# Another order for the rounds of a graph attention: where VectorE's and TensorE's pieces of work stand between the links of a chain

## The chip, the cores and the metric

One core of one Trainium2 chip runs the whole kernel as one program. The metric is device time in microseconds; the kernel before was run three times, 1138.68, 1143.45 and 1144.17 us, so its median is 1143.45 us. One more execution was recorded by the hardware profiler; it took 1135.31 us, with a span of 1133.6 us from the first to the last instruction.

## The reference

The reference is one layer of a graph network on 3125 nodes of 256 features and 50000 edges, sorted by their destination node. Three parts are added to the input: an attention over the edges, a linear attention over all nodes, and a mixture of eight experts. Only the first is touched here:

```
q = (feats @ Wq.T + bq)   k = (feats @ Wk.T + bk)   v = (feats @ Wv.T + bv)     # 8 heads of 32
qe = q[:, c, :]    ke = k[:, r, :]    ve = v[:, r, :]      # r: source, c: destination of each edge
sim = einsum('hed,hed->eh', qe, ke) * scale
m = segment_max(sim, c)          p = exp(sim - m[c])       s = segment_sum(p, c)
out_e = (p / s[c]) * ve          agg = segment_sum(out_e, c)
return agg @ Wo.T + bo
```

So for each edge and each head there is a product of the destination's query with the source's key, a softmax over the edges that share a destination, and a weighted sum of the sources' values.

## The kernel before, in words

The program has stages one after another: preparation (projections, tables of the edges), the linear attention, the edge attention (function `attention`, from about 200 to 815 us), and the end with the experts. The five engines each have an instruction stream of their own, which runs in the order in which it is written, and they meet by semaphores only. There is no scheduler: the order of the code is the order on the engine.

In `attention` the edges are cut into 28 chunks of 16 steps of 128 edges (the last chunk has 8 steps). A step is one row of tiles: 128 edges on the partitions, all in the window of one block of 125 nodes. Four steps are a turn (q = 0 to 3), so a chunk has four turns. For each turn the work is:

- GpSimd gathers the keys and values of the source nodes with 4 indirect DMAs (L968) into one of ten ring places.
- `turned_hots(n)` on VectorE (L1048) makes the one-hot matrix hotT of a whole chunk; `spread_q(n, q)` on TensorE (12 matmuls, L1194) multiplies it with the node queries, so that each edge has its query in the PSUM tile at_pq (two of them, by turns).
- `product(n, q)` on VectorE (L1054) multiplies at_pq with the gathered keys, `reduce(n, q)` (L1061) sums each head: the scores.
- `turn_scores(c)` on TensorE transposes the scores of a chunk, and a chain of small steps finds the maximum of each node's edges, also across rows and chunks: `local_maxima` (two scans on VectorE, L1096 and L1098), `ends` (two transposes on TensorE), a copy on ScalarE (at_row, L1022), `carries` (two scans of one row and three small operations on VectorE, L1102 to L1107), `columns` (TensorE L1221, then VectorE's copy L1111), `maxima` (L1115, L1117, L1119), the exponential on ScalarE (L1030), `turn_weights` and `factor` on TensorE (L1227, L1232).
- `weigh(c, q)` on VectorE (L1070) multiplies the values with the weights into at_pv; `sums(c, q)` on TensorE (two groups of 4 matmuls, L1204) sums over the edges of each node; `add(c, q, i)` on VectorE (L1084) adds each group's result to the node sums agg; `rescale(c)` (L1092) multiplies a node's sums when its maximum has grown.

ScalarE also makes the one-hot matrices at_hot for `sums` (L988, L991).

A round n works on three chunks at once: the scores of chunk n, the chain and the first two turns of the sums of chunk c = n - 1, and the last sums of chunk b = n - 2. The order of the pieces within a round is written out by hand in the function `body` of each engine. Two things set what may start: `spread_q(n, q)` may overwrite a tile at_pq only when the product two turns back is done, and group p of `sums` may overwrite its tile only when the add two groups back is done. `windows(c, q)` loads the numbers of the node blocks of a turn from a table into registers (L929, TENSOR_LOAD); the instructions that address agg by them (add and rescale) have a short register instruction ahead (shown as ISA).

Of the kernel before, what the change touches and what calls it, by code (L numbers as in the profile page):

```python
# [862 lines left out]
def attention(nc, m):  # L863
# [7 lines left out]
    with ExitStack() as ctx:  # L871
# [43 lines left out]
        def exists(c, q=0):  # L915

            return not isinstance(c, int) or (0 <= c < CH and q < quads(c))
# [15 lines left out]
        with nc.Block() as block:  # L933
# [109 lines left out]
            def _(dve):  # L1043
# [65 lines left out]
                def columns(c):  # L1109
                    dve.wait_ge(S.chain_pe, CHAIN_PE * c + PE_COLUMNS)  # L1110
                    dve.tensor_copy(col[:, :], pc[:, 384:386]).then_inc(S.chain, 1)  # L1111
# [9 lines left out]
                def body(n):  # L1121
                    c, b = n - 1, n - 2
                    if exists(b, 2):
                        weigh(b, 2)
                    if exists(b, 1):
                        wins = windows(b, 1)
                        add(b, 1, 0, wins)
                    if exists(n, 0):
                        product(n, 0)
                    if exists(b, 1):  # L1130
                        add(b, 1, 1, wins)
                    if exists(c):
                        local_maxima(c)
                    if exists(n, 0):
                        reduce(n, 0)
                    if exists(c):
                        carries(c)

                    if exists(b, 3):
                        weigh(b, 3)  # L1140
                    if exists(b, 2):
                        wins = windows(b, 2)
                        add(b, 2, 0, wins)
                    if exists(c):
                        columns(c)
                    if exists(b, 2):
                        add(b, 2, 1, wins)
                    if exists(c):
                        maxima(c)
                    if exists(n, 1):  # L1150
                        product(n, 1)
                        reduce(n, 1)

                    if exists(c, 0):
                        weigh(c, 0)
                    if exists(b, 3):
                        wins = windows(b, 3)
                        add(b, 3, 0, wins)
                    if exists(n, 2):
                        product(n, 2)  # L1160
                    if exists(b, 3):
                        add(b, 3, 1, wins)
                    if exists(n, 2):
                        reduce(n, 2)
                    if exists(c):
                        wins = windows(c, 0)
                        rescale(c, wins[0])

                    if exists(c, 1):
                        weigh(c, 1)  # L1170
                    if exists(c, 0):
                        add(c, 0, 0, wins)
                    if exists(n) and exists(n + 1):
                        turned_hots(n + 1)
                    if exists(c, 0):
                        add(c, 0, 1, wins)
                    if exists(n, 3):
                        product(n, 3)
                        reduce(n, 3)
                turned_hots(0)  # L1180
                dve.wait_ge(S.at_const, AT_CONST)
# [4 lines left out]
            def _(pe):  # L1186
# [47 lines left out]
                def windows(c, q):  # L1234
                    return windows_of(c, slice(2 * q, 2 * q + 2), PE_ONLY)

                def body(n):
                    c, b = n - 1, n - 2
                    if exists(n, 1):
                        wins = windows(n, 1)  # L1240
                    if exists(n, 1):
                        spread_q(n, 1, wins)
                    if exists(n, 2):
                        wins = windows(n, 2)
                    if exists(c):
                        turn_scores(c)
                    if exists(b, 2):
                        sums(b, 2)
                    if exists(c):
                        ends(c)  # L1250

                    if exists(c):
                        columns(c)
                    if exists(n, 2):
                        spread_q(n, 2, wins)
                    if exists(n, 3):
                        wins = windows(n, 3)
                    if exists(b, 3):
                        sums(b, 3)
                    if exists(c):  # L1260
                        turn_weights(c)
                        factor(c)

                    if exists(n, 3):
                        spread_q(n, 3, wins)
                    if exists(n) and exists(n + 1):
                        wins = windows(n + 1, 0)
                    if exists(c, 0):
                        sums(c, 0)

                    if exists(c, 1):
                        sums(c, 1)
                    if exists(n) and exists(n + 1):
                        spread_q(n + 1, 0, wins)
                pe.wait_ge(S.at_const, AT_CONST)
                spread_q(0, 0, windows_of(0, slice(0, 2), PE_ONLY))
                for n in range(CH + 2):
# [598 lines left out]
```

## Time and profile before

| | us |
|---|---|
| median of three runs (1138.68 to 1144.17) | 1143.45 |
| profiled execution | 1135.31 |
| its span | 1133.6 |
| VectorE busy | 867.7 |
| TensorE busy (matmul) | 893.9 |
| GpSimd busy | 586.7 |
| ScalarE busy | 484.7 |

The span is longer than any engine's busy time because the stages have different limits. VectorE is busy for 90% and more in the slices of the attention and for less than half in the experts, TensorE is busy for 70 to 80% in the attention and for over 90% in the experts. The mean clock granted to TensorE is 0.916 of full speed over the whole span. A matmul's busy time includes the time in which it overlaps the next, so a sum of such times is no measure of work.

### The profile page before, as it was taken

What the parts mean: (1) busy time and instruction counts of PE and PEld (TensorE: products, weight loads), DVE (VectorE), ACT (ScalarE), POOL (GpSimd) and SP (SyncE); (2) the same over time, 40 slices, a digit from 0 to 9 for tenths busy, and PEclk for the clock granted to TensorE, in tenths of its full rate; (3) what the DMA queues carried; (4) which work ended last, traced back from release to release, by engine and by line L of the source; (5) the groups of instructions that cost most, each with busy time, mean ns of one, the idle gap of its engine ahead of it and who ended that gap; (6) DMA issues with size and microseconds to landing.
All of it is one profiled execution on the core that took longest, in us unless ns stands there. A gap on an engine that the chain in (4) does not pass through costs nothing. (4 is left out here: it accounts for less than half of the span.)

```text
span 1133.6 us, 15267 instructions
## 1 busy us (share of the span) xinstructions
PE 893.9 (79%) x4059; PEld 618.0 (55%) x4059; DVE 867.7 (77%) x1760; ACT 484.7 (43%) x1312; POOL 586.7 (52%) x635
## 2 busy tenths in 40 slices
PE   4889967578777777777877877777685599999995
PEld 3445543356556555555555655555453366666664
DVE  3787877799999999999999999999578134444444
ACT  3566436454455454445445445544332232232330
POOL 2533467767777777777777777771001323232311
PEclk9989969788998988999989899997887799999998
DMA  5334265468777777777677676671231443333300
GB/s 147 107 98 112 78 178 153 146 188 216 217 203 210 213 204 189 191 199 201 184 199 194 176 197 181 174 201 44 68 111 63 132 149 120 103 121 114 111 11 9
DMA packets 79878, 167.46 MB, mean 148 GB/s; under 512 B 15514, under 2 KB 47005, under 8 KB 79549
## 3 DMA queue, kind: packets, MB, share of 16 engines
q0 software_dynamic: 38464, 110.26, 36.2%
q1 hardware_dynamic: 39431, 54.81, 15.6%
q10 hardware_dynamic: 1904, 1.45, 0.4%
q8 instruction: 35, 0.57, 0.2%
q14 instruction: 44, 0.36, 0.1%
HBM read 163.32 MB, written 18.95 MB: 161 GB/s over the span
## 5 line engine op out<-in xcount | busy, mean ns | idle before, releaser
L968 POOL DMA_INDIRECT slot<-kv_d,src_e x320 | 322.8, 1009 | 116.3 <-issue 91.7
L1204 PE MATMUL at_pa<-at_pv,at_hot 128*125 128x264 f32 x880 | 268.0, 446 | 81.4 <-DVE agg L1084 80.5
L1204 PEld LDWEIGHTS at_pa<-at_pv,at_hot 128*125 128x125 f32 x880 | 173.6, 213 | 155.1 <-DVE agg L1084 126.4
L988 ACT ACTIVATE at_hot<-iota_w,nloc_e 128x125 f32<-128x125 f32 x440 | 138.9, 386 | 132.8 <-PE at_pa L1204 132.6
L1194 PE MATMUL at_pq<-q,at_hotT 125*128 x1320 | 172.2, 287 | 16.0 <-issue 10.9
L1194 PEld LDWEIGHTS at_pq<-q,at_hotT 125*128 125x128 bf16 x1320 | 130.5, 102 | 44.5 <-issue 20.5
L1061 DVE TENSOR_REDUCE at_sc<-at_prod 128x32 f32<-128x1024 f32 x110 | 133.4, 1213 | 2.0
L1635 DVE TENSOR_TENSOR y<-xp,b 128x256 f32<-128x256 f32 (+1 forms) x32 | 13.6, 425 | 138.3 <-PE xp L1681 138.3
L1614 POOL DMA_INDIRECT out<-slot,node_s x32 | 32.1, 1004 | 166.0 <-DVE slot L1646 135.3
L1054 DVE TENSOR_TENSOR at_prod<-at_pq,slot 128x1024 f32<-128x1024 f32 x88 | 107.0, 1216 | 9.3 <-PE at_pq L1194 7.0
L1681 PE MATMUL xp<-slot,hm 128*128 128x256 f32 (+1 forms) x512 | 113.1, 379 | 0.0
L1070 DVE TENSOR_TENSOR at_pv<-slot,at_pp 128x1056 f32<-128x1056 f32 x88 | 109.3, 1242 | 0.0
L1671 PE MATMUL xp<-extra,slot 128*128 128x489 f32 x256 | 108.2, 581 | 0.8 <-ACT extra L1579 0.8
L1681 PEld LDWEIGHTS xp<-slot,hm 128*128 128x128 f32 (+1 forms) x512 | 94.3, 185 | 18.2 <-issue 3.5
L1084 DVE TENSOR_TENSOR agg<-agg,at_pa 125x264 f32 x220 | 92.4, 420 | 8.0 <-PE at_pa L1204 3.0
L1590 ACT ACTIVATE hm<-xp,b 128x489 f32<-128x489 f32 x64 | 42.9, 670 | 114.2 <-PE xp L1671 114.2
L991 ACT ACTIVATE at_hot<-at_hot,one_col 128x500 f32<-128x500 f32 x110 | 78.3, 712 | 3.6
L1671 PEld LDWEIGHTS xp<-extra,slot 128*128 128x128 f32 x256 | 49.3, 193 | 55.5 <-issue 49.7
L1221 PE MATMUL at_pchain<-at_one_c,at_line 1*128 1x1 f32 x112 | 17.3, 254 | 48.2 <-DVE at_line L1105 48.2
L631 PE MATMUL pa<-slot,xnT 128*125 128x512 f32 x100 | 51.1, 637 | 3.8 <-DVE vst L438 3.8
L968 POOL DMA_INDIRECT base<-kv_d,src_e x44 | 44.5, 1012 | 14.2 <-issue 12.3
L968 POOL DMA_INDIRECT extra<-kv_d,src_e x44 | 44.0, 1001 | 14.7 <-issue 12.8
(319 smaller groups left out, 1318.4 us busy)
## 6 DMA issues: line engine op xcount, KB each, us to landing
slot<-in_w SPq DMA_DIRECT2D x16, 1024.0 KB, 7.6
locrow<-loc_d SPq DMA_DIRECT2D x28, 500.0 KB
slot<-kv_d,src_e POOLq DMA_INDIRECT x352, 4.0
kv_d<-vst SPq DMA_DIRECT2D x25, 128.9 KB
base<-in_x SPq DMA_DIRECT2D x5, 625.0 KB
kv_d<-kst SPq DMA_DIRECT2D x25, 125.0 KB
row_d<-base SPq DMA_DIRECT2D x5, 625.0 KB
out<-base SPq DMA_DIRECT2D x1, 3125.0 KB
```

The costliest lines, as they stand in the source:

```text
L631: mm = pe.matmul(dst[par][0:TT, 0:b - a], xnT[:, par, c, :], wall[:, c, a:b], start=(c == 0), stop=(c == 1))
L968: pool.indirect_dma_start(m.quads[r][:, i, :], None, m.kv_d, bass.IndirectOffsetOnAxis(ap=m.src_e[:, c, u:u + 1].bitcast(U32), axis=0), bo ...
L988: last = act.activation(hot[:, u % 8, :], m.iota_w[:, :], ACT.Abs, bias=at(m.nloc_e, c)[:, u:u + 1])
L991: act.activation(hot[:, four, :], hot[:, four, :], ACT.Relu, bias=m.one_col[:, 0:1], scale=-1.0).then_inc(S.hot_made, 1)
L1054: dve.tensor_tensor(prod[:, :, :], pq[q % 2].rearrange("p (i d) -> p i d", i=4), m.quads[place(n, q)][:, :, 0:D], ALU.mult).then_inc(S.pro ...
L1061: dve.tensor_reduce(sc[:, :, 4 * q:4 * q + 4].rearrange("p h i -> p i h"), prod.rearrange("p i (h d) -> p i h d", h=H), X, ALU.add).then_i ...
L1070: dve.tensor_tensor(pv[:, 4 * (q % 2):4 * (q % 2) + 4, :, :], m.quads[place(c, q)][:, :, D:KV].rearrange("p i (h c) -> p i h c", h=H), spr ...
L1084: dve.tensor_tensor(dst, dst, pa[p % 2][:, 0:H * VW].rearrange("p (h c) -> p h c", h=H), ALU.add).then_inc(S.added, 1)
L1194: mm = pe.matmul(pq[q % 2][:, u * D:(u + 1) * D], hotT[:, 4 * q + u, :], at(m.q3, wins[u // 2])[:, part, :], start=(part == 0), stop=(part ...
L1204: mm = pe.matmul(pa[p % 2][:, 0:H * VW], hot[:, u % 8, :], pv[:, u % 8, :, :].rearrange("p h c -> p (h c)"), start=(u % 2 == 0), stop=(u % ...
L1671: mm = pe.matmul(p1[f % 2][:, 0:CAP], w1[par][:, c, f * 128:(f + 1) * 128], hT[par][:, c, 0:CAP], start=(c == 0), stop=(c == 1))
L1681: mm = pe.matmul(p2[i % 2][0:sizes[i], 0:D], hm[:, f, 128 * i:128 * i + sizes[i]], w2[par][:, f, :], start=(f == 0), stop=(f == FC - 1))
```

## The change

The functions that do the work are not touched. In the rounds of VectorE, `carries(c)` moves behind `weigh(b, 3)` and the first add of turn 2, `product(n, 1)` and `reduce(n, 1)` move ahead of `columns(c)` and `maxima(c)` and have an add between them, the adds of turn 3 follow `maxima(c)` at once, `turned_hots(n + 1)` moves ahead of `weigh(c, 0)`, `weigh(c, 0)` moves behind it, and `product(n, 3)` and `reduce(n, 3)` have an add between them. In the rounds of TensorE, `turn_scores(c)` goes ahead of `spread_q(n, 1)`, `ends(c)` ahead of `sums(b, 2)`, `columns(c)` goes behind `spread_q(n, 2)`, `turn_weights(c)` and `factor(c)` behind `spread_q(n, 3)`, and `spread_q(n + 1, 0)` ahead of `sums(c, 0)`.

```diff
--- before.py
+++ after.py
@@ -1131,28 +1131,27 @@
                         add(b, 1, 1, wins)
                     if exists(c):
                         local_maxima(c)
+
                     if exists(n, 0):
                         reduce(n, 0)
-                    if exists(c):
-                        carries(c)
-
                     if exists(b, 3):
                         weigh(b, 3)
                     if exists(b, 2):
                         wins = windows(b, 2)
                         add(b, 2, 0, wins)
                     if exists(c):
-                        columns(c)
+                        carries(c)
+
+                    if exists(n, 1):
+                        product(n, 1)
                     if exists(b, 2):
                         add(b, 2, 1, wins)
+                    if exists(n, 1):
+                        reduce(n, 1)
                     if exists(c):
+                        columns(c)
                         maxima(c)
-                    if exists(n, 1):
-                        product(n, 1)
-                        reduce(n, 1)
-
-                    if exists(c, 0):
-                        weigh(c, 0)
+
                     if exists(b, 3):
                         wins = windows(b, 3)
                         add(b, 3, 0, wins)
@@ -1162,20 +1161,23 @@
                         add(b, 3, 1, wins)
                     if exists(n, 2):
                         reduce(n, 2)
+                    if exists(n) and exists(n + 1):
+                        turned_hots(n + 1)
+
+                    if exists(c, 0):
+                        weigh(c, 0)
                     if exists(c):
                         wins = windows(c, 0)
                         rescale(c, wins[0])
-
                     if exists(c, 1):
                         weigh(c, 1)
                     if exists(c, 0):
                         add(c, 0, 0, wins)
-                    if exists(n) and exists(n + 1):
-                        turned_hots(n + 1)
+                    if exists(n, 3):
+                        product(n, 3)
                     if exists(c, 0):
                         add(c, 0, 1, wins)
                     if exists(n, 3):
-                        product(n, 3)
                         reduce(n, 3)
                 turned_hots(0)
                 dve.wait_ge(S.at_const, AT_CONST)
@@ -1238,40 +1240,39 @@
                     c, b = n - 1, n - 2
                     if exists(n, 1):
                         wins = windows(n, 1)
+                    if exists(c):
+                        turn_scores(c)
                     if exists(n, 1):
                         spread_q(n, 1, wins)
                     if exists(n, 2):
                         wins = windows(n, 2)
                     if exists(c):
-                        turn_scores(c)
+                        ends(c)
                     if exists(b, 2):
                         sums(b, 2)
-                    if exists(c):
-                        ends(c)
-
-                    if exists(c):
-                        columns(c)
+
                     if exists(n, 2):
                         spread_q(n, 2, wins)
                     if exists(n, 3):
                         wins = windows(n, 3)
+                    if exists(c):
+                        columns(c)
                     if exists(b, 3):
                         sums(b, 3)
-                    if exists(c):
-                        turn_weights(c)
-                        factor(c)
-
                     if exists(n, 3):
                         spread_q(n, 3, wins)
                     if exists(n) and exists(n + 1):
                         wins = windows(n + 1, 0)
+                    if exists(c):
+                        turn_weights(c)
+                        factor(c)
+
+                    if exists(n) and exists(n + 1):
+                        spread_q(n + 1, 0, wins)
                     if exists(c, 0):
                         sums(c, 0)
-
                     if exists(c, 1):
                         sums(c, 1)
-                    if exists(n) and exists(n + 1):
-                        spread_q(n + 1, 0, wins)
                 pe.wait_ge(S.at_const, AT_CONST)
                 spread_q(0, 0, windows_of(0, slice(0, 2), PE_ONLY))
                 for n in range(CH + 2):
```

The first place is on VectorE, from the carries' end to the first add of turn 3 (agg<-agg,at_pa is an add, at_prod a product, at_sc a reduce, at_pv a weigh, win_of the table of windows). Before:

```order
L1111 COPY at_col<-at_pchain 128x2 [waits chain_pe]
L1084 ISA [waits added,summed]
L1084 TENSOR_TENSOR agg<-agg,at_pa 125x264
L1115 SCALAR_TENSOR_TENSOR at_fwd_max<-edge,at_col,at_pchain 128x128 [waits chain]
L1117 SCALAR_TENSOR_TENSOR at_back_max<-at_bwd_st,at_col,at_fwd_max 128x128 [waits chain]
L1119 TENSOR_TENSOR at_back_max<-at_pchain,at_back_max 128x128 [waits chain]
L1054 TENSOR_TENSOR at_prod<-at_pq,extra 128x1024 [waits reduced,q_spread,arrived9]
L1061 TENSOR_REDUCE at_sc<-at_prod 128x4x8 [waits prod_made]
L1070 TENSOR_TENSOR at_pv<-slot,at_pp 128x1056 [waits summed,chain_pe]
L929 TENSOR_LOAD win_of
L1084 ISA [waits added,summed]
L1084 TENSOR_TENSOR agg<-agg,at_pa 125x264
```

and now, from the reduce of turn 1 on:

```order
L1061 TENSOR_REDUCE at_sc<-at_prod 128x4x8 [waits prod_made]
L1111 COPY at_col<-at_pchain 128x2 [waits chain_pe]
L1115 SCALAR_TENSOR_TENSOR at_fwd_max<-edge,at_col,at_pchain 128x128 [waits chain]
L1117 SCALAR_TENSOR_TENSOR at_back_max<-at_bwd_st,at_col,at_fwd_max 128x128 [waits chain]
L1119 TENSOR_TENSOR at_back_max<-at_pchain,at_back_max 128x128 [waits chain]
L929 TENSOR_LOAD win_of
L1084 ISA [waits added,summed]
L1084 TENSOR_TENSOR agg<-agg,at_pa 125x264
L1054 TENSOR_TENSOR at_prod<-at_pq,slot 128x1024 [waits reduced,q_spread,arrived0]
```

The table load (L929) stood behind a product, a reduce and a weigh; now it stands directly behind the three instructions of maxima, each of which waits on the semaphore `chain` for the one before, and the adds that need it come next.

The second place is on VectorE too, in the second half of a round, about hotT. Before:

```order
L1061 TENSOR_REDUCE at_sc<-at_prod 128x4x8 [waits prod_made]
L929 TENSOR_LOAD win_of
L1092 ISA [waits added,chain_pe]
L1092 TENSOR_TENSOR agg<-agg,at_pchain 125x264
L1070 TENSOR_TENSOR at_pv<-slot,at_pp 128x1056 [waits summed]
L1084 TENSOR_TENSOR agg<-agg,at_pa 125x264 [waits added,summed,rescaled]
L1048 TENSOR_SCALAR at_hotT<-locrow,iota_p 125x2048 [waits q_spread,loc_in]
L1084 ISA [waits added,summed,rescaled]
L1084 TENSOR_TENSOR agg<-agg,at_pa 125x264
```

and now:

```order
L1061 TENSOR_REDUCE at_sc<-at_prod 128x4x8 [waits prod_made]
L1048 TENSOR_SCALAR at_hotT<-locrow,iota_p 125x2048 [waits q_spread,loc_in]
L1070 TENSOR_TENSOR at_pv<-slot,at_pp 128x1056 [waits summed,chain_pe]
L929 TENSOR_LOAD win_of
L1092 ISA [waits added,chain_pe]
L1092 TENSOR_TENSOR agg<-agg,at_pchain 125x264
L1070 TENSOR_TENSOR at_pv<-slot,at_pp 128x1056 [waits summed]
L1084 TENSOR_TENSOR agg<-agg,at_pa 125x264 [waits added,summed,rescaled]
L1054 TENSOR_TENSOR at_prod<-at_pq,slot 128x1024 [waits reduced,q_spread,arrived1]
L1084 ISA [waits added,summed,rescaled]
L1084 TENSOR_TENSOR agg<-agg,at_pa 125x264
```

hotT stood between the two adds of turn 0 of chunk c, behind weigh and rescale; now it stands ahead of the weigh, and two weighs and the rescale are all that is between it and the first of those adds.

The third place is on TensorE, from the turn of the weights to the turn of the scores (at_pp is the turned weights, at_pchain<-at_fall the factor, at_pq a spread, at_pa sums; each spread has twelve matmuls, and rows that repeat are left out). Before:

```order
L1227 MATMUL at_pp<-ident,at_back_max 128x128 [waits pv_made,chain_act]
L1232 MATMUL at_pchain<-at_fall,at_pair 125x8 [waits chain,chain_act]
L1194 ISA [waits prod_made]
L1194 MATMUL at_pq<-q,at_hotT 128x256
...
L929 TENSOR_LOAD win_of
L1204 MATMUL at_pa<-at_pv,at_hot 125x264 [waits pv_made,hot_made,added]
L1204 MATMUL at_pa<-at_pv,at_hot 125x264
...
L1204 MATMUL at_pa<-at_pv,at_hot 125x264 [waits pv_made,hot_made,added]
...
L1194 ISA [waits prod_made,hotT_made]
```

and now:

```order
L1229 MATMUL at_pp<-ident,at_back_max 128x128 [waits pv_made,chain_act]
L1234 MATMUL at_pchain<-at_fall,at_pair 125x8 [waits chain,chain_act]
L1196 ISA [waits prod_made,hotT_made]
L1196 MATMUL at_pq<-q,at_hotT 128x256
...
L1206 MATMUL at_pa<-at_pv,at_hot 125x264 [waits pv_made,hot_made,added]
L1206 MATMUL at_pa<-at_pv,at_hot 125x264
...
L1206 MATMUL at_pa<-at_pv,at_hot 125x264 [waits pv_made,hot_made,added]
...
L1213 MATMUL at_pchain<-ident,at_sc 128x128 [waits rescaled,reduced]
L1196 ISA [waits prod_made]
```

Before, the spread that waits for hotT stood behind the sums of turns 0 and 1; now it stands ahead of them, and they can't start until it has been through. Line numbers on TensorE are two higher in the changed kernel.

## Rows read from the trace of the kernel before

**Rows 1.** The instructions on the tile hotT in the attention (xcount: ns min/median/max, first and last start).

```profile
L1048 DVE TENSOR_SCALAR at_hotT<-locrow,iota_p x26: 744/758/768, 234.4 to 775.1; 125x2048 bf16<-125x2048 bf16 x26
```

**Rows 2.** Busy time by engine in 25 rounds (stretch, length, busy us (x count), clock, DMA).

```profile
234.40:775.10 540.70, 417.39 (x2250) 303.45 (x2250) 523.18 (x826) 263.48 (x728) 400.57 (x398) 0.93 0.73 197
```

**Rows 3.** VectorE's waits in that stretch (waiting line <- releaser: us, times, longest).

```profile
DVE at_run L1102 <- ACT at_row L1022: 4.6, 10, 0.5
DVE at_prod L1054 <- issue: 2.8, 10, 0.4
```

**Rows 4.** VectorE's timeline, about one round (start us, us, instruction).

```profile
537.99 0.75 DVE L1048 TENSOR_SCALAR at_hotT<-locrow,iota_p 125x2048 bf16<-125x2048 bf16 x1
...
544.99 1.19 DVE L1061 TENSOR_REDUCE at_sc<-at_prod 128x32 f32<-128x1024 f32 x1
546.30 0.45 DVE L1102 TENSOR_TENSOR_SCAN at_run<-at_stop,at_row 1x144 f32<-1x144 bf16 x1
...
549.06 0.14 DVE L1111 COPY at_col<-at_pchain 128x2 f32<-128x2 f32 x1
549.34 0.43 DVE L1084 TENSOR_TENSOR agg<-agg,at_pa 125x264 f32 x1
549.69 0.47 DVE L1115 TENSOR_TENSOR_SCAN at_fwd_max<-edge,at_col,at_pchain 128x128 f32<-128x128 bf16 x1
...
550.72 0.29 DVE L1119 TENSOR_TENSOR at_back_max<-at_pchain,at_back_max 128x128 f32<-128x128 f32 x1
550.93 1.22 DVE L1054 TENSOR_TENSOR at_prod<-at_pq,slot 128x1024 f32<-128x1024 f32 x1
552.18 1.22 DVE L1061 TENSOR_REDUCE at_sc<-at_prod 128x32 f32<-128x1024 f32 x1
553.31 1.24 DVE L1070 TENSOR_TENSOR at_pv<-slot,at_pp 128x1056 f32<-128x1056 f32 x1
554.47 0.42 DVE L1084 TENSOR_TENSOR agg<-agg,at_pa 125x264 f32 x1
554.81 1.22 DVE L1054 TENSOR_TENSOR at_prod<-at_pq,slot 128x1024 f32<-128x1024 f32 x1
555.95 0.42 DVE L1084 TENSOR_TENSOR agg<-agg,at_pa 125x264 f32 x1
...
559.25 0.77 DVE L1048 TENSOR_SCALAR at_hotT<-locrow,iota_p 125x2048 bf16<-125x2048 bf16 x1
```

**Rows 5.** GpSimd's gathers in the stretch, by group (busy, mean ns | idle before, releasers).

```profile
L968 POOL DMA_INDIRECT slot<-kv_d,src_e x318 | 320.8, 1009 | 109.3 <-issue 91.4 <-DVE at_pv L1070 17.9
L968 POOL DMA_INDIRECT base<-kv_d,src_e x40 | 40.5, 1012 | 13.1 <-issue 11.4 <-DVE at_pv L1070 1.8
L968 POOL DMA_INDIRECT extra<-kv_d,src_e x40 | 40.0, 1000 | 13.5 <-issue 11.6 <-DVE at_pv L1070 1.9
```

**Rows 6.** TensorE's waits, its longest gap among them.

```profile
PE at_pchain L1221 <- DVE at_line L1105: 43.0, 25, 1.9
```

**Rows 7.** Busy time and granted clock in two neighbouring stretches.

```profile
557.00:560.40 3.40, 1.58 (x7) 0.82 (x5) 3.40 (x7) 1.98 (x5) 2.69 (x3) 1.00 0.23 52
560.40:563.80 3.40, 3.40 (x13) 2.36 (x13) 3.37 (x3) 1.26 (x4) 2.59 (x3) 0.51 0.74 158
```

**Rows 8.** VectorE's timeline in the last rounds, an add and the rescale behind it.

```profile
792.95 0.43 DVE L1084 TENSOR_TENSOR agg<-agg,at_pa 125x264 f32 x1 [0.21 <-DVE agg L1084]
793.73 0.43 DVE L1092 TENSOR_TENSOR agg<-agg,at_pchain 125x264 f32 x1 [0.35 <-DVE agg L1084]
```

**Rows 9.** TensorE's timeline, spread and sums at the low clock and at the full one.

```profile
227.99 2.74 PE L1194 MATMUL at_pq<-q,at_hotT 125*128 x12
...
330.46 1.51 PE L1194 MATMUL at_pq<-q,at_hotT 125*128 x12
...
513.31 1.16 PE L1204 MATMUL at_pa<-at_pv,at_hot 128*125 128x264 f32 x4 [0.32 <-DVE agg L1084]
...
787.00 3.88 PE L1204 MATMUL at_pa<-at_pv,at_hot 128*125 128x264 f32 x8 [1.00 <-DVE agg L1084]
```

## The prediction

> **What bounds the kernel now.** I read the attention stage first, because only its rounds are touched. The row of the hotT instruction [rows 1] gives the round: 26 of them stand between 234.4 and 775.1 us, so 25 rounds take (775.1 - 234.4) / 25 = 21.63 us each. The row of that stretch [rows 2] shows VectorE busy for 523.18 of 540.70 us, TensorE for 417.39, and a granted TensorE clock of 0.93 on average. VectorE's waits in the same stretch [rows 3] are 4.6 and 2.8 us, small against the whole. So VectorE is the bound, and a round is the sum of the distances from start to start of its instructions. Those I take from one round of its timeline [rows 4]: hotT to hotT is 559.25 - 537.99 = 21.26 us in an undisturbed round, and the other 0.37 us of the mean are waits of TensorE's late work.
>
> GpSimd is close behind. In the same stretch it waited for VectorE's weighings (at_pv) for 17.9 + 1.8 + 1.9 = 21.6 us [rows 5] and had gathers or their issue in the rest. With 16 gathers a round, 400 in all, one needs (540.7 - 21.6) / 400 = 1.30 us, and a round 20.8 us. Below 20.8 us no order of VectorE's work brings anything.
>
> TensorE has slack, and this is where its clock comes in. It waited for VectorE in gaps of at most 1.9 us [rows 6], several in each round. What such a gap does is in two rows [rows 7]: from 557.0 to 560.4 TensorE was busy 1.58 of 3.40 us, at clock 1.00 (2.4 GHz); from 560.4 to 563.8, fully busy, it was granted 0.51, which is the 1.2 GHz level. The average of 0.93 says that this happens in about one part in seven of the time.
>
> **The change part by part: VectorE's own sum.** No instruction is added or removed; every round issues the same ones. Four distances change.
> 1. carries(c) now stands behind weigh(b,3) and add(b,2,0). Before, the first scan of carries started 1.31 us after the reduce (546.30 - 544.99) [rows 4], while a reduce followed by work that is ready takes 1.13 (553.31 - 552.18). The 0.18 us was the wait for the turned ends and ScalarE's copy. With 1.16 + 0.34 us more in between it goes: -0.18.
> 2. product and reduce of turns 1 and 3 had stood next to each other: 1.25 us from one to the other (552.18 - 550.93), against 1.14 from a product to an add (555.95 - 554.81). Now an add stands between both pairs: 2 x 0.11 = -0.22.
> 3. columns(c) had add(b,2,1) behind it: 0.28 + 0.35 us (549.06, 549.34, 549.69) [rows 4]. Now the scan follows the 0.14 us copy directly. It waits for the copy to end, about 0.18 us, and the add costs its 0.34 elsewhere: 0.63 - 0.52 = -0.11.
> 4. windows(b,3), a load of a table entry into a register, now stands directly behind maxima, whose instructions each wait for the one before. An instruction that addresses by the loaded value can't start before it. In the last rounds of before the same pair stands uncovered [rows 8]: from the add at 792.95 to the rescale at 793.73 it takes 0.78 us instead of 0.34, and the idle time before it is 0.35. The rescale's register instruction waits there for the add to end too, but the add is over after 0.43; the rest is the load. The same 0.78 behind the last instruction of maxima, where the next one now starts after 0.21 (550.93 - 550.72) [rows 4], costs 0.57 us. It can cost nothing if the load starts under the scans; it cannot gain. I take +0.57, because the last step of maxima waits for a semaphore as the add of [rows 8] does. In before this load lay under a weigh of 1.24 us.
>
> Sum: 21.26 - 0.18 - 0.22 - 0.11 + 0.57 = 21.32 us. So VectorE's own work is no shorter than in an undisturbed round of today.
>
> The Trainium skill ("Perfetto Trace Analysis", section "DVE / Act Engine Instruction") has an instruction with a wait pushed into a wait queue, and the sequencer free for the next instruction at once. By that rule the load would start under the scans and item 4 would be 0, the sum 20.75. The row at 793.73 speaks against it for an add's wait; no row of before shows it for a scan's.
>
> **What TensorE does to it.** The new order of TensorE puts spread_q(n+1,0) ahead of sums(c,0), and turned_hots(n+1), which it waits for, comes late on VectorE: only weigh(c,0), rescale and weigh(c,1) stand between hotT and add(c,0,0), which needs the first sums. From the start of hotT that is 0.69 (its 0.77 less the overlap of 0.08 that a weigh shows too: 1.24 long, the next starts after 1.16) + 1.16 + 0.34 + 1.16 = 3.35 us [rows 4]. TensorE needs in that time: hotT's own 0.77, about 0.1 to start, 12 spread matmuls (1.51 us, of which 1.3 until the next can stream) and 4 matmuls of sums (1.16 us when alone, 1.1 behind others) [rows 9]: 3.3 us. At the full clock it fits by nothing. At the low level the same 12 took 2.74 us and 8 of sums 3.88, so 4 take 1.94 [rows 9]: 2.6 + 1.9 = 4.5 instead of 2.4, and add(c,0,0) is late by 2.1 us, with product(n,3), the next add and the reduce queued behind it on VectorE.
>
> Which clock will it be? TensorE's work in the new order ends with factor(c): the scans of maxima end at about 11.6 us after weigh(b,2), ScalarE and the turn take 0.7, factor 0.4: 12.7. hotT ends at about 15.8. In between TensorE has nothing that may start: spread_q(n+1,0) waits for hotT, sums(c,0) stands behind it. That is a gap of 3.1 us in every round, where before the longest was 1.9 [rows 6] and the half empty stretch of [rows 7] was enough to lose the clock. So I expect the low level during just this spread and these sums in nearly every round. The low stretch of [rows 7] lasted 3.4 us and the work at that level takes 4.5, so where it starts inside the gap and is granted anew the add is late by the full 2.1, where it starts in the work only for its rest. The bounds are 0 (the full clock) and 2.1 (always low); I take 1.5, nearer to the low rows.
>
> A second place: sums(b,2) wait behind ends(c), which wait for local_maxima. From the backward scan to add(b,2,0) VectorE has 0.31 + 1.13 + 1.16 = 2.6 us; the scan's end (0.39), the two turns (0.45) and 4 matmuls (1.1) take 1.95. At the low level that is about 3.1, late by 0.5 or 0.6. TensorE idles for 2 us ahead of it (between spread_q(n,1) and ends), so I expect that in a third of the rounds: +0.2, bounds 0 and 0.6.
>
> The other moves are covered: columns and turn_weights are done on TensorE over 1.5 and 3 us before VectorE asks for them; the chunk's gathers and the table DMA keep their places, and a longer round gives them more time.
>
> **The sum.** 21.32 + 1.5 + 0.2 = 23.0 us a round, 1.37 more than 21.63. Times 25 rounds: +34 us. The first and the last rounds change by perhaps 2 us either way, taken as 0. The profiled execution took 1135.31 us (1133.6 of span and 1.7 around it), so it would take 1169.6. The median of the runs, 1143.45, stands 8.1 above the profiled execution; on that scale the forecast is 1177 us.
>
> **The rivals.**
> - Faster: the load hides under the scans (item 4 is 0) and the clock holds through the gap. Place: the stretch from maxima to add(c,0,0). Then VectorE needs 20.75, GpSimd 20.8, the round is 20.8, 25 x 0.83 = 21 us less: 1122. It decides from the point where both waits are under 0.3 us together. For it: the gathers leave room and every chain wait of [rows 3] goes. Against: [rows 8] and [rows 7]. The skill's rule above gives this time.
> - The clock holds but the load is paid: 21.32 us, 8 us less, 1135. Against it: the gap is longer than any today.
> - Clock low in few rounds, 0.4 us on average: 21.7, +2 us, 1145. For it: today's gaps cost the clock only in some rounds.
> - Worse than forecast: the clock stays low on through the next ends and sums(b,2), so all of 2.1 + 0.6 and some of sums of turn 3, 24.5 us: +72, 1215. For it: a longer round empties TensorE further. Against: at the low level TensorE's work takes nearly the whole round, which fills it.
> - The change doing nothing to the order can be left aside: the rows of the built program show it.
>
> **How the numbers follow.** Forecast 0.65, worse 0.10, few rounds low 0.10, load paid and clock held 0.05, faster with both hidden 0.10. The time is the forecast's, 1177. Its own range, from a late add of 0.9 to 2.1 us, is 1160 to 1193. For 8 in 10 the range reaches down to 1147, by the same argument for smaller lateness, and up to 1195. A measurement tells about 0.5% (5.7 us) from no change. Slower: 0.65 + 0.10 + a part of the few-rounds case = 0.78; within: 0.08; faster: 0.14.
>
> **What would show it.** In the new trace hotT to hotT is 23.0 us. VectorE waits before add(c,0,0) for sums, 1.5 us in the mean, and before the first add of turn 3 0.55 us under "issue" or with the scan as releaser, in each round. TensorE waits over 2.5 us for hotT, and its clock in the rounds is below 0.90. The wait for ScalarE's row copy is gone. Wrong would be: a round near 21 us, GpSimd without waits for at_pv, or a clock of 0.93 or more in spite of the gap.

## The result, and the profile after

The changed kernel took 1166.7 us (median of 4 runs, 1156.1 to 1168.16), the kernel before 1141.07 us on the same chip (4 runs). The ratio is 1.019, with a 95% interval of 1.015 to 1.023: slower by 22 us in that ratio, 26 in the medians. The forecast was 1177 us and slower.

The profiled execution of the changed kernel has a span of 1165.9 us. VectorE's hotT instructions, TensorE's and VectorE's busy time in 25 rounds, and what the engines waited for there, answer to [rows 1 to 3] and [rows 5, 6]:

```profile
L1048 DVE TENSOR_SCALAR at_hotT<-locrow,iota_p x26: 743/745/911, 237.9 to 805.0; 125x2048 bf16<-125x2048 bf16 x26
```

```profile
237.90:805.00 567.10, 432.18 (x2250) 319.40 (x2250) 518.59 (x826) 263.16 (x729) 400.96 (x400) 0.88 0.68 188
```

```profile
DVE agg L1084 <- issue: 42.2, 43, 2.1
DVE agg L1084 <- PE at_pa L1206: 2.3, 5, 1.5
```

```profile
PE at_pq L1196 <- DVE at_hotT L1048: 74.8, 25, 3.4
PE at_pchain L1217 <- DVE at_back_max L1098: 48.8, 25, 2.0
```

```profile
POOL slot L968 <- DVE at_pv L1070: 47.9, 30, 9.3
```

The round is (805.0 - 237.9) / 25 = 22.68 us, against 21.63 [rows 1]: 1.05 us more, 26.3 us in 25 rounds. VectorE was busy for 518.6 of 567.1 us; before it was for 523.2 of 540.7, so its idle time grew from 17.5 us to 48.5. Its waits are now all before adds: 42.2 us put down to "issue" and 2.3 to the sums. The word "issue" stands for idle time in which the profile names no releaser. Before an add it covers two things here: the table load, and waits for the sums that a sequencer instruction ahead of the add takes upon itself. TensorE waited 74.8 us for hotT, 3.0 a round, and its mean clock fell from 0.93 to 0.88. The two spans differ by 32.3 us, not 26.3: 6.9 of it is the start of the attention (first hotT at 208.6 us instead of 201.7), which lies ahead of everything that was changed. Of the ten profiled executions of this study four had it at 201.7 to 202.5 us and six at 207.0 to 208.9; b1 below, which has the changed order of TensorE, is among the early ones. What decides it stays open. The times of one kernel fall into two groups in the same way (b1: 1117.88 and 1118.42, then 1127.24 and 1127.37), probably by this start, so that a median of four can move by several us without any change in the rounds. GpSimd waited for the weighings for 60.8 us in all (47.9 of it in the row above), against 21.6 before [rows 5], so it is further from being the bound.

One round on VectorE, which answers to [rows 4] and [rows 8], shows where the idle time stands:

```profile
485.54 0.74 DVE L1048 TENSOR_SCALAR at_hotT<-locrow,iota_p 125x2048 bf16<-125x2048 bf16 x1
...
487.70 1.25 DVE L1070 TENSOR_TENSOR at_pv<-slot,at_pp 128x1056 f32<-128x1056 f32 x1
491.02 0.43 DVE L1084 TENSOR_TENSOR agg<-agg,at_pa 125x264 f32 x1 [2.07 <-issue]
491.37 1.22 DVE L1054 TENSOR_TENSOR at_prod<-at_pq,slot 128x1024 f32<-128x1024 f32 x1
...
497.58 1.20 DVE L1061 TENSOR_REDUCE at_sc<-at_prod 128x32 f32<-128x1024 f32 x1
498.69 1.25 DVE L1070 TENSOR_TENSOR at_pv<-slot,at_pp 128x1056 f32<-128x1056 f32 x1
...
505.32 0.29 DVE L1119 TENSOR_TENSOR at_back_max<-at_pchain,at_back_max 128x128 f32<-128x128 f32 x1
506.10 0.43 DVE L1084 TENSOR_TENSOR agg<-agg,at_pa 125x264 f32 x1 [0.48 <-issue]
```

and on TensorE, from hotT on, the same stretch (it answers to [rows 9]), first a round with the low clock, then one with the full clock:

```profile
486.43 2.74 PE L1196 MATMUL at_pq<-q,at_hotT 125*128 x12 [3.42 <-DVE at_hotT L1048]
488.96 5.17 PE L1206 MATMUL at_pa<-at_pv,at_hot 128*125 128x264 f32 x16
...
509.93 1.51 PE L1196 MATMUL at_pq<-q,at_hotT 125*128 x12 [2.81 <-DVE at_hotT L1048]
511.27 1.06 PE L1206 MATMUL at_pa<-at_pv,at_hot 128*125 128x264 f32 x4
```

In the first, hotT (485.54, 0.74 long) lets the spread start at 486.43, after 3.42 us in which TensorE had nothing to do. The 12 matmuls take 2.74 us, which is their length at 1.2 GHz [rows 9], the sums follow at 488.96, and the add that should have started at 487.70 + 1.16 = 488.86 starts at 491.02: 2.16 us late. The semaphore of these sums was raised at 490.94 in the trace, so the add did wait for the sums, though its row says "issue". In the second the gap is 2.81, the spread 1.51 and the first sums 1.06, and nothing is late. The step from the last instruction of maxima (505.32) to the add (506.10) is 0.78 us, with an idle time of 0.47 to 0.49, in each round. The load, which these rows leave out, starts 0.013 to 0.015 us after the start of that last instruction and takes 0.53 us. The clock in the gap and behind it (it answers to [rows 7]; columns as there):

```profile
483.00:486.40 3.40, 0.01 (x1) 0.00 (x0) 3.40 (x5) 2.90 (x8) 2.79 (x3) 0.70 0.73 188
486.40:489.80 3.40, 3.37 (x14) 2.55 (x15) 2.55 (x3) 0.00 (x0) 2.00 (x3) 0.50 0.76 170
```

TensorE was busy for 0.01 us of the first stretch, and the clock fell within it, so that its mean is 0.70; it was 0.50 in the next, in which TensorE worked without a break. The other rounds say the same. Between the end of hotT and the time at which the add of turn 0 is due, the granted clock was 1.00 in the 6 rounds in which the add was late by 0.22 us at most, and 0.50 to 0.81 in the 20 in which it was late by 1.0 us or more.

### The profile page after: what moved, and what is told of

The parts are those of the page before. It is cut to its first block and busy times, and to the rows that moved or that the text cites. A ratio compares the mean times of both kernels' runs of the same rounds, so it can differ in the third digit from the quotient of the medians.

```text
span 1165.9 us, 15267 instructions
## 1 busy us (share of the span) xinstructions
PE 908.4 (78%) x4059; PEld 634.7 (54%) x4059; DVE 865.6 (74%) x1760; ACT 484.4 (42%) x1312; POOL 583.5 (50%) x635
## 5 line engine op out<-in xcount | busy, mean ns | idle before, releaser
L1206 PE MATMUL at_pa<-at_pv,at_hot 128*125 128x264 f32 x880 | 262.9, 450 | 7.1 <-DVE at_pv L1070 3.6
L1196 PE MATMUL at_pq<-q,at_hotT 125*128 x1320 | 192.8, 303 | 91.4 <-DVE at_hotT L1048 80.6
L1206 PEld LDWEIGHTS at_pa<-at_pv,at_hot 128*125 128x125 f32 x880 | 183.5, 221 | 58.4 <-DVE agg L1084 17.8
L1196 PEld LDWEIGHTS at_pq<-q,at_hotT 125*128 125x128 bf16 x1320 | 138.9, 107 | 133.0 <-issue 99.9
L1217 PE MATMUL at_pchain<-ident,at_fwd_max 128*1 128x128 f32 x28 | 7.6, 271 | 52.1 <-DVE at_back_max L1098 51.9
```

The lines of the kernel that those rows point to most:

```text
L1196: mm = pe.matmul(pq[q % 2][:, u * D:(u + 1) * D], hotT[:, 4 * q + u, :], at(m.q3, wins[u // 2])[:, part, :], start=(part == 0), stop=(part ...
L1206: mm = pe.matmul(pa[p % 2][:, 0:H * VW], hot[:, u % 8, :], pv[:, u % 8, :, :].rearrange("p h c -> p (h c)"), start=(u % 2 == 0), stop=(u % ...
```

## The experiments

Theory 1: two costs make the loss. The table load directly behind maxima is paid in full, and the gap of 3 us on TensorE ahead of spread_q(n+1,0) takes its clock away, so that the spread and the sums that VectorE waits for run at half speed. The rivals: the path hotT, spread, sums, add is too long at any clock; or TensorE, not VectorE, sets the round, and what one cost gives back the other takes.

**f1_filler: work in the gap.** 18 matmuls whose result is overwritten by the spread behind them.

```diff
                     if exists(n) and exists(n + 1):
+                        if exists(c):
+                            pe.wait_ge(S.prod_made, QUADS * (n + 1) - 1)
+                            for _ in range(18):
+                                pe.matmul(pq[0][:, 0:D], m.q3[:, 0, 0, 0:128], m.q3[:, 1, 0, :], start=True, stop=True)
                         spread_q(n + 1, 0, wins)
```

> The changed kernel with 18 extra matmuls (results overwritten, never read) on TensorE in each round, in the gap between product(n,2) and hotT, ahead of spread_q(n+1,0). Theory 1 (the gap costs the clock, and the low clock makes the spread and the sums late): the gap is mostly filled, the granted clock of the rounds rises from 0.88 to 0.93 or more, add(c,0,0) is late by 0.3 us or less instead of 1.3 on average, a round is 21.4 to 21.7 us instead of 22.7, the time 1137 to 1146 us. Theory 2 (the path hotT, spread, sums, add is too long at any clock): the add stays late by 1.3 us, the time stays at 1160 us or more.

Measured: 1130.0 us, ratio to the kernel before 0.989 (0.984 to 0.995), 37 us less than the changed kernel in the medians. Its TensorE with the filler, in one round:

```profile
302.55 2.14 PE L1274 MATMUL at_pq<-q 125*128 125x256 bf16 x18 [0.47 <-DVE at_prod L1054]
304.76 1.51 PE L1196 MATMUL at_pq<-q,at_hotT 125*128 x12
306.11 2.84 PE L1206 MATMUL at_pa<-at_pv,at_hot 128*125 128x264 f32 x12
```

```profile
L1048 DVE TENSOR_SCALAR at_hotT<-locrow,iota_p x26: 742/744/746, 236.8 to 774.7; 125x2048 bf16<-125x2048 bf16 x26
```

```profile
DVE agg L1084 <- issue: 14.1, 26, 1.4
```

The round is (774.7 - 236.8) / 25 = 21.52 us. VectorE's waits for "issue" fell from 42.2 us to 14.1 in nearly the same number of rounds, and about 11.5 of that are the load, 24 times 0.48. The add of turn 0 was late by 1.4 to 1.7 us in 3 of 26 rounds, with a granted clock of 0.70 to 0.74 in front of it, and by 0.15 at most in the other 23, with a clock of 1.00. So nearly all of the late add was the clock: the same order, with the same gap for useful work, loses 1.2 us a round when TensorE stands still in it. Theory 2 of the expectation is out. That work added to an engine makes the kernel 3% faster is the plainest sign of it. The round came out as expected, but the time is 7 us below the expected range. The profiled execution itself took 1137.29 us, the longest of the four, so its trace does not show where the other three gained 6 to 10 us; a start of the attention at 202 instead of 207 us would be 5 of it.

**f2_filler_short: a third of the filler.** As f1, `range(6)`.

> As f1_filler, with 6 extra matmuls a round instead of 18: TensorE works for 0.65 us more in the gap, which leaves about 1.5 us behind them and 0.9 ahead. Theory 1 (the share of the gap that is empty decides): a part of the rounds keep the full clock; the late add costs 0.6 to 1.1 us a round, the round is 21.9 to 22.4, the time 1145 to 1160, between the changed kernel's and that of f1. Rival (any matmul in the gap is enough to keep the clock): as f1, 21.5 us and 1130 to 1137.

Measured: 1155.4 us, ratio 1.014 (1.009 to 1.019), the round (793.7 - 237.1) / 25 = 22.26 us. VectorE's waits for "issue" were 28.5 us, between f1's and the changed kernel's. In the single rounds of its trace the add of turn 0 was late by 1.5 to 2.2 us in 13 of 26 and by 0.1 in the others: it is nearly all or nothing, as the low stretch falls on the spread or not (the granted clock ahead of the add was 0.50 to 0.67 in the 13 late rounds and 1.00 in the others). The rival, that any matmul keeps the clock, is out.

**l1_load_early: the load ahead of the scans.**

```diff
                         reduce(n, 1)
+                    if exists(b, 3):
+                        wins = windows(b, 3)
                     if exists(c):
                         columns(c)
                         maxima(c)
                     if exists(b, 3):
-                        wins = windows(b, 3)
                         add(b, 3, 0, wins)
```

> The changed kernel with the load of windows(b,3) issued ahead of columns and maxima instead of behind them. Theory 1 (the load is paid in full where nothing covers it): the step from the last instruction of maxima to the first add of turn 3 falls from 0.77 to 0.21 us, 0.55 us a round; the wait for the sums keeps its length, since hotT and the add move together, so a round is 22.1 us and the time 14 us less, 1150 to 1155. Rival (TensorE, not VectorE, sets the round once its clock is low): what the load gives back is taken by a longer wait before add(c,0,0), the round stays within 0.2 us of 22.7 and the time above 1160.

Measured: 1147.0 us (10 runs), ratio 1.004 (1.001 to 1.007). VectorE at the place, and the hotT row:

```profile
497.76 0.29 DVE L1119 TENSOR_TENSOR at_back_max<-at_pchain,at_back_max 128x128 f32<-128x128 f32 x1
497.97 0.42 DVE L1084 TENSOR_TENSOR agg<-agg,at_pa 125x264 f32 x1
```

```profile
L1048 DVE TENSOR_SCALAR at_hotT<-locrow,iota_p x26: 741/743/745, 238.2 to 785.9; 125x2048 bf16<-125x2048 bf16 x26
```

The add starts 0.21 us after the last instruction of maxima. The round is (785.9 - 238.2) / 25 = 21.91, 0.77 less than in the changed kernel: 0.55 for the load, and 0.2 because the add of turn 0 was late by less. I had expected that wait to keep its length, so the time came out 3 us below the expected range. The rival, that the gain is taken back by TensorE, is out.

**m1_load_in_before: the load put there in the old order.** One line of the kernel before is moved, and nothing else.

```diff
                         maxima(c)
+                    if exists(b, 3):
+                        wins = windows(b, 3)
                     if exists(n, 1):
                         product(n, 1)
                         reduce(n, 1)
                     ...
                     if exists(b, 3):
-                        wins = windows(b, 3)
                         add(b, 3, 0, wins)
```

> The kernel before with one line moved: the load of windows(b,3) directly behind maxima, ahead of product(n,1), the rest in the old order. Theory 1 (a table load behind an instruction that waits for the one before is paid in full): the step from the last instruction of maxima to product(n,1) grows from 0.21 to 0.77 us, a round from 21.63 to 22.2, the time by 14 us to about 1156. Rival (the 0.55 us are hidden by waits that today's order has anyway, for ScalarE's row or the spread): a round grows by 0.2 or less, the time by under 5 us.

Measured: 1156.9 us, ratio 1.016 (1.011 to 1.021), the round (791.5 - 235.1) / 25 = 22.26 us. The place on VectorE:

```profile
492.83 0.29 DVE L1119 TENSOR_TENSOR at_back_max<-at_pchain,at_back_max 128x128 f32<-128x128 f32 x1
493.52 1.23 DVE L1054 TENSOR_TENSOR at_prod<-at_pq,slot 128x1024 f32<-128x1024 f32 x1 [0.40 <-issue]
```

Here the instruction behind the load is a product, which does not use what is loaded, and it waits all the same: 0.69 us instead of 0.21. So the load stops the stream of VectorE, not just its user. It explains 0.48 of the 0.63 us; the rest came as more rounds in which the product of turn 0 and the row copy were late (13 of 25 instead of 10), the wait of [rows 3].

**v1_vector_only: VectorE's new order with TensorE's old one.** The body of TensorE's rounds is that of the kernel before, the rest is the changed kernel.

> VectorE's new order with TensorE's old one: the sums of turns 0 and 1 stand ahead of spread_q(n+1,0) again. Theory 1 (the spread ahead of the sums puts hotT on the path of the add): nothing waits for hotT, but the weigh of turn 0 now comes so late that TensorE's gap moves in front of the sums and is about 3 us long; the sums run at the low clock in most rounds, add(c,0,0) is late by 0.3 to 0.6 and the second add by some more, the round is 22.0 to 22.3 us, the time 1150 to 1157. Rival (the spread's place is the whole loss): the round is 21.3, VectorE's own sum, and the time 1134 or less.

Measured: 1151.1 us (10 runs), ratio 1.009 (1.005 to 1.013), the round (783.7 - 233.4) / 25 = 22.01 us. TensorE's waits:

```profile
PE at_pchain L1223 <- DVE at_line L1105: 61.5, 24, 2.6
PE at_pa L1206 <- DVE at_pv L1070: 55.9, 23, 3.0
```

and one of VectorE's:

```profile
DVE at_prod L1054 <- issue: 6.4, 8, 1.1
```

Nothing waits for hotT, but the gap has moved: TensorE waits 55.9 us for weigh (up to 3.0), ahead of the sums, and 61.5 us for carries (up to 2.6). So VectorE's new order already makes a long gap, 2.4 us on average against 3.0 in the changed kernel; TensorE's new order decides what stands behind it. The time and the round were as expected, but the place of the loss was not: the add of turn 0 was late in 4 rounds of 26 only, by 0.92 us, which is 0.15 on average instead of 0.3 to 0.6. The largest part is the product of turn 0, which waited up to 1.1 us in 8 rounds for the spread behind the slow sums, and in 3 rounds the first add of turn 3 was late by about 1 us. That the sum fits is luck in part.

**s1_sums_first: the first sums ahead of the spread.** As the changed kernel, with `sums(c, 0)` before `spread_q(n + 1, 0)` in TensorE's rounds and `sums(c, 1)` behind it.

```diff
-                    if exists(n) and exists(n + 1):
-                        spread_q(n + 1, 0, wins)
                     if exists(c, 0):
                         sums(c, 0)
+                    if exists(n) and exists(n + 1):
+                        spread_q(n + 1, 0, wins)
                     if exists(c, 1):
```

> The changed kernel with sums(c,0) ahead of spread_q(n+1,0) on TensorE and sums(c,1) behind it. Theory 1: the first sums wait for the weigh alone; the gap on TensorE grows to 4 us, so they run at the low clock, 4 matmuls in 1.94 instead of 1.1 us, and add(c,0,0) is late by 0.6 us, the next add by 0.3: a round of 22.1 to 22.3, time 1150 to 1157, less than the changed kernel's 1167 by half of its loss. Rival (the place of the spread is all of it): a round of 21.3, 1134.

Measured: 1166.4 us, ratio 1.021 (1.017 to 1.025), no better than the changed kernel, so this expectation missed by 9 us. The round is (781.0 - 237.9) / 24 = 22.63 us. TensorE and then VectorE in one round:

```profile
489.21 3.85 PE L1206 MATMUL at_pa<-at_pv,at_hot 128*125 128x264 f32 x8 [4.58 <-DVE at_pv L1070]
492.86 2.05 PE L1196 MATMUL at_pq<-q,at_hotT 125*128 x12
```

```profile
489.32 1.25 DVE L1070 TENSOR_TENSOR at_pv<-slot,at_pp 128x1056 f32<-128x1056 f32 x1
491.40 0.43 DVE L1084 TENSOR_TENSOR agg<-agg,at_pa 125x264 f32 x1 [0.83 <-issue]
491.75 1.22 DVE L1054 TENSOR_TENSOR at_prod<-at_pq,slot 128x1024 f32<-128x1024 f32 x1
493.27 0.43 DVE L1084 TENSOR_TENSOR agg<-agg,at_pa 125x264 f32 x1 [0.30 <-PE at_pa L1206]
```

The gap is 4.58 us, and the 8 matmuls behind it took 3.85 us, the length at the low clock. The add of turn 0 is late by 2.08 - 1.16 = 0.92 us, in all 26 rounds, and the next by 0.4 (from 491.75 to 493.27, 1.52 instead of 1.13) in 16 of them and by less in the others. I had priced the two at 0.9 together; they were 1.2 on average, and the sums of turn 1 behind them made the first add of the next round late too, by 0.2 on average. Here a path that is shorter by a whole spread gained nothing, because the gap ahead of it was longer.

**h1_hots_early: hotT 1.5 us sooner.**

```diff
                         product(n, 2)
+                    if exists(n) and exists(n + 1):
+                        turned_hots(n + 1)
                     if exists(b, 3):
                         add(b, 3, 1, wins)
                     if exists(n, 2):
                         reduce(n, 2)
-                    if exists(n) and exists(n + 1):
-                        turned_hots(n + 1)
```

> The changed kernel with turned_hots(n+1) behind product(n,2) instead of behind reduce(n,2), 1.5 us sooner, so that spread_q(n+1,0) can start 2 us sooner, at the end of product(n,2). Theory 1: TensorE's gap shrinks from 3.1 to 1.1 us, a second of 1.8 us comes before the sums, the clock is near that of before (0.92 or more), add(c,0,0) is late by 0.2 us on average, the round is 21.4 to 21.6 us, the time 1135 to 1144. Rival (the clock falls just the same, in the gap before the sums): the sums alone are late by 0.6 to 0.9, the round is 22.0, the time 1150.

Measured: 1143.3 us (10 runs), ratio 1.001 (0.997 to 1.004): the whole loss is gone with this one move, though the load is still paid. The round is (780.9 - 237.8) / 25 = 21.72 us, 0.1 above what I expected; the add was late by 0.8 to 1.0 us in 11 of 26 rounds (0.4 on average, where I had expected 0.2) and in time in most of the others. TensorE's 3 us are now two waits, one for hotT (1.8 us at most) and one for the weigh (1.1 at most). The clock did not come back as I had expected: it was 0.90 on average between 240 and 760 us, not 0.92 or more. But the spread is now done before the weigh, so that a low stretch makes the add late by 0.9 us where it was 2.2 in the changed kernel.

**b1_both_early: both moves.** The edits of l1 and h1 together.

> The changed kernel with both moves: the load of windows(b,3) ahead of columns, and turned_hots(n+1) behind product(n,2). Theory 1: both costs go, VectorE's own sum is 20.75 us and GpSimd's 20.8 us become the bound, with some rounds late at the low clock: 20.9 to 21.2 us a round, 11 to 18 us less than before, 1123 to 1130. Rival (GpSimd's gathers already bind sooner than its row says, or the clock takes it back): 21.4 us or more, no faster than before, 1138 or above.

Measured: 1122.8 us, ratio to the kernel before 0.985 (0.978 to 0.992), faster than both kernels. Busy time in the rounds, VectorE's and GpSimd's waits:

```profile
237.90:760.00 522.10, 409.76 (x2242) 299.99 (x2240) 513.93 (x822) 262.29 (x725) 400.64 (x398) 0.93 0.73 203
```

```profile
DVE agg L1084 <- issue: 3.3, 5, 0.8
DVE agg L1084 <- PE at_pa L1207: 1.0, 4, 0.3
```

```profile
POOL slot L968 <- DVE at_pv L1070: 1.8, 6, 0.3
```

```profile
L1048 DVE TENSOR_SCALAR at_hotT<-locrow,iota_p x26: 741/743/746, 231.8 to 756.7; 125x2048 bf16<-125x2048 bf16 x26
```

The round is (756.7 - 231.8) / 25 = 21.00 us, VectorE is busy for 513.9 of 522.1 us, and GpSimd has stopped waiting for VectorE: 1.8 us in all, where before it was 21.6 [rows 5]. Its gathers follow each other at 1.30 us, which is 20.8 us a round, so rounds below that could not go on for long. That GpSimd alone is now the bound is not shown: VectorE is at its limit too, and none of its waits is for a gather.

The trace shows another tie between the two. In the rounds of b1 without a late add, 20.63 us is the shortest and 20.85 the most frequent length, and the difference is one small copy of carries (L1105, 256 values on one partition), which takes 0.52 instead of 0.28 us. It depends on where it meets a gather. In the ten traces 50 of these copies started 0.53 to 0.76 us after the start of a gather, and 49 of them took 0.51 to 0.55 us and one 0.40; none of the other 207 took more than 0.34. In b1 it was long in 12 of 28 rounds, in the changed kernel in one, in the kernel before in 10, where it is part of the 0.37 us a round that the prediction had put down to TensorE's late work.

## Why the prediction was right

The direction and the mechanism held; two of the terms were too large, so that the time was 10 us above the measured one, inside the range. Some 8 us of that are the two terms, and 2.4 the median of the kernel before, 1143.45 us in the prediction and 1141.07 beside the result.

- VectorE's own sum: forecast 21.32 us. The shortest round of the changed kernel took 21.26. The three savings came: from the reduce at 497.58 to what follows 1.11 us instead of 1.31, from a product to the add behind it 1.13, from the column copy to the scan 0.17 and the add elsewhere. The load cost 0.78 - 0.21 = 0.57, as priced; l1 and m1 took it away and put it in. So item 4 of the change was shown by experiment, and the rule of the Trainium skill ("Perfetto Trace Analysis", section "DVE / Act Engine Instruction"), by which the sequencer is free for the next instruction while one waits, did not hold here: the load behind the scans starts only 0.013 to 0.015 us after the last instruction of maxima has started, in every round of the changed kernel and of m1.
- The late add of turn 0: forecast 1.5 us a round between bounds of 0 and 2.1. It was late by 2.16 us at most, which is the upper bound, and by 1.36 on average over 26 rounds: in 6 of them it was late by 0.22 at most, though there was a gap of 2.7 us or more in each. My "nearly every round" was too much. f1, which fills the gap, and f2, which has a third of its filler, show the cause, and the granted clock of the single rounds parts the late from the others without exception.
- The sums of turn 2 behind ends: forecast 0.2. In the trace the weigh ahead of that add was followed late in 4 of 25 rounds, by 0.3 us at most, 0.03 on average. This term was mis-sized. The low clock was there about as often as I had put it, in 9 of 25 rounds, in which the 4 matmuls took 1.4 to 2.0 us instead of 1.05. The length of the path was wrong: I had put 3.1 us for it at the low level. It was 0.45 us from the start of the backward scan to the two turns, 0.22 from there to the sums and 2.0 at most for these, 2.6 or 2.7 in all, and VectorE needs 2.6 itself.
- The sum: 1.05 us a round were measured, 1.37 forecast, of which some 0.15 is the late add of turn 0 and 0.17 the sums of turn 2. From the first hotT to the last add of the attention the changed kernel took 27.1 us more, so the first and last rounds, taken as 0, were 0.8.
- The forecast's own range: with a late add of 0.9 us its sum is 22.42 us a round, which is 1163 us; the 1160 in the prediction is 3 too low.
- The rivals: that the load would hide and the clock hold is ruled out by each trace, but it names the version that b1 is: 1122 us was its price and 1122.8 was measured, with a round of 21.00 us instead of 20.8. That the times agree to 1 us is luck, since the four times of b1 are 1118 and 1127 in pairs.
- The signs listed: hotT to hotT 22.7 instead of 23.0, the wait for ScalarE's row copy gone, 0.48 us of "issue" before the first add of turn 3, 3.0 us of waiting for hotT a round, a clock of 0.88. The late add of turn 0, too, stands mostly under "issue" and not under the sums as forecast.

## What to carry to other kernels

An order that gives the bounding engine shorter distances can still lose: ask what the other engine's gaps become. On TensorE one gap of 3 us cost more here than several of 1 to 2, because what stood behind it then ran at half speed in 20 of 26 rounds (a spread took 2.74 instead of 1.51 us). Try to split such a gap, by an operand made sooner (h1), before making the path behind it shorter (s1). A register load belongs behind a long instruction whose waits are over by then, since it stops the stream of its engine: 0.78 us from maxima to the add instead of 0.21.

## What the runs showed that I had not expected

Added work helped: 18 useless matmuls a round made the changed kernel 3% faster (f1). It was also 1% faster than the kernel before, but the rounds of its trace account for only 2.7 of those 13 us (21.52 us against 21.63). And the mean granted clock alone tells little: it was 0.95 in the rounds of both f1 and f2,

```profile
237.90:760.00 522.10, 440.51 (x2630) 329.90 (x2629) 502.31 (x800) 255.00 (x704) 391.04 (x387) 0.95 0.72 198
```

```profile
237.90:760.00 522.10, 400.88 (x2253) 292.64 (x2254) 487.72 (x773) 246.90 (x680) 376.45 (x375) 0.95 0.70 192
```

while their rounds differ by 0.74 us. Between 240 and 760 us TensorE spent the same 51.2 us at the low level in both. In f1 it fell on the spread and the sums ahead of the add in 3 of 26 rounds, in f2 in 13. What counts is whether the low stretches fall on the work that another engine waits for.
